# A cross-attention kernel whose media preparation is cut into four chunks and spread over four engines, with part of the value projection behind the first scores

## The reference

```python
qn = layernorm(x, ln_q_g, ln_q_b)
q = qn @ Wq * scale
k, v = jnp.split(media @ Wkv, 2, axis=-1)
sim = jnp.einsum('bhid,bhjd->bhij', q, k)
sim = jnp.where(media_mask[:, None, None, :], sim, neg_inf)
attn = jax.nn.softmax(sim, axis=-1)
out = jnp.einsum('bhij,bhjd->bhid', attn, v)
x = x + jnp.tanh(attn_gate) * attn_out
```

## Time and profile before

| | us |
|---|---|
| median of 3 runs | 939.61 (937.93 to 944.74) |
| the profiled execution, its own time | 945.04 |
| its span | 943.2 |
| TensorE busy | 860.3 (91%) |
| VectorE busy | 610.4 (65%) |
| ScalarE busy | 442.6 (47%) |
| GpSimd busy | 393.1 (42%) |

### The profile page before, as it was taken

How to read it: one execution, slowest core, us unless ns; L and a number is a source line. 1 busy time by engine, 2 the same in 40 slices (tenths; PEclk the granted TensorE clock), 3 DMA queues, 4 the chain that set the end, 5 groups by cost and what they waited for, 6 DMA issues and landing times.

```text
span 943.2 us, 18307 instructions
## 1 busy us (share of the span) xinstructions
PE 860.3 (91%) x7811; PEld 720.0 (76%) x7811; DVE 610.4 (65%) x941; ACT 442.6 (47%) x663; POOL 393.1 (42%) x179
## 2 busy tenths in 40 slices
PE   3589999999999999999999999999998789967996
PEld 2488887788888878888887888888876568846884
DVE  5766798968658888775788868666865132442243
ACT  2255545655445556454554655445544231414141
POOL 0035555556635655555555556635655400000000
PEclk9689999999999999999999999999999899988999
DMA  7100001000000100000000000000024000002000
GB/s 250 33 1 2 1 1 37 1 1 2 1 1 1 36 2 2 2 1 1 2 1 1 2 1 2 1 1 1 2 60 135 1 1 1 1 23 69 0 0 22
DMA packets 19629, 16.61 MB, mean 18 GB/s; under 512 B 849, under 2 KB 18658, under 8 KB 19426
## 3 DMA queue, kind: packets, MB, share of 16 engines
q1 hardware_dynamic: 19554, 15.51, 5.4%
HBM read 14.46 MB, written 1.05 MB: 16 GB/s over the span
## 4 chain that ended last, share of the span: by engine, by line
PE 78%; DVE 11%; ACT 4%; POOL 3%; issue 2%; DMA 2%; SPq 1%; DVEq 0%; POOLq 0%; ACTq 0%
PE psum L910 20%; PE psum L924 16%; PE psum L313 14%; PE psum L881 6%; PE psum L847 4%; PE psum L947 3%; PE psum L980 3%; PE psum L989 3%; PE psum L1035 2%; POOL acc L404 2%; DVE mx L663 2%; PE psum L940 1%; DVE k_lo L656 1%; ACT v L466 1%; DMA wq<-in_L_xattn_Wq_dram 1%
## 5 line engine op out<-in xcount | busy, mean ns | idle before, releaser
L404 POOL TENSOR_TENSOR acc<-acc,ring 128x1024 f32<-128x1024 f32 x128 | 306.5, 2394 | 18.7 <-POOL acc L404 0.4
L663 DVE TENSOR_REDUCE mx<-psum 128x2 f32<-128x800 f32 (+2 forms) x256 | 245.3, 990 | 85.3 <-PE psum L881 77.8
L481 ACT ACTIVATE ring<-psum 128x1024 f32<-128x1024 f32 x192 | 197.0, 1027 | 77.3 <-PE psum L910 71.0
L399 POOL TENSOR_TENSOR acc<-ring 128x1024 f32<-128x1024 f32 x32 | 76.7, 2398 | 322.8 <-ACT ring L481 322.8
L924 PE MATMUL psum<-ring,v 128*64 128x256 f32 (+1 forms) x1664 | 186.7, 381 | 1.8
L924 PEld LDWEIGHTS psum<-ring,v 128*64 128x64 f32 (+1 forms) x1664 | 116.7, 137 | 60.6 <-DVE k_lo L656 3.9
L910 PE MATMUL psum<-nm,maskrow 64*128 64x256 f32 (+1 forms) x832 | 125.9, 298 | 2.2 <-DVE maskrow L645 1.6
L910 PE MATMUL psum<-q_hi,k_hi 64*128 64x256 f32 (+1 forms) x832 | 119.2, 282 | 0.0
L910 PE MATMUL psum<-q_lo,k_hi 64*128 64x256 f32 (+1 forms) x832 | 118.8, 281 | 0.0
L910 PE MATMUL psum<-q_hi,k_lo 64*128 64x256 f32 (+1 forms) x832 | 118.6, 280 | 0.0
L881 PE MATMUL psum<-k_hi,q_hi 64*128 64x400 f32 (+1 forms) x512 | 97.2, 378 | 12.9 <-DVE mx L663 8.3
(11 more groups left out here) (149 smaller groups left out, 1366.6 us busy)
## 6 DMA issues: line engine op xcount, KB each, us to landing
nat<-in_ctx_dram SPq DMA_DIRECT2D x8, 768.0 KB
w<-in_L_xattn_W_dram SPq DMA_DIRECT2D x2, 1024.0 KB, 7.9
xs<-in_x_dram SPq DMA_DIRECT2D x4, 256.0 KB, 5.3
ring<-in_L_xattn_Wkv_dram SPq DMA_DIRECT2D x1, 1024.0 KB, 7.2
wq<-in_L_xattn_Wq_dram SPq DMA_DIRECT2D x1, 1024.0 KB, 9.3
wo<-in_L_xattn_Wo_dram SPq DMA_DIRECT2D x1, 1024.0 KB, 10.3
out_dram<-t_res SPq DMA_DIRECT2D x4, 256.0 KB, 2.2
mask<-in_mask_BxS_bk_dram SPq DMA_DIRECT2D x4, 200.1 KB, 5.9
```

The lines of the kernel that those rows point to most:

```text
L399: nc.gpsimd.tensor_tensor(acc[:, :, :, :], ring[:, 0, :, :, :], ring[:, 1, :, :, :], ALU.add)\
L404: nc.gpsimd.tensor_tensor(acc[:, :, :, :], acc[:, :, :, :], ring[:, g, :, :, :], ALU.add)\
L481: nc.scalar.activation(ring[:, g, :, :, :], score_set[m % 2].rearrange("p (h i q) -> p h i q", h=2, i=2), ACT.Exp).then_inc(S["p_ready"], 1)
L663: nc.vector.tensor_reduce(mx[:, t, :, c], aux_pair[BANK[item] // 2][:, :, 0:min(c1, KEYS) - c0], axis=AX.X, op=ALU.max).then_inc(S["m_max" ...
```

## The change

The media preparation is cut into four chunks of 400 columns (those of K) in place of two halves. The sum over the columns is taken by ScalarE in five parts, each as the accumulator output of a copy of one T part, whose copy (`unread`) nobody reads; VectorE then adds up five numbers. The mixing of the mean is an item of its own (`Y`, four parts), and `P` has four parts. The weights' low parts are made by GpSimd. The mask row is written by ScalarE. K.8.c waits for its own chunk of `mt_lo` and for `wk_lo` alone; V.4 waits for `wv_lo`. The DMA of x and those of the norm rows are issued by ScalarE; SyncE's queue is mask, media, the K half of Wkv, Wq, the V half, Wo. In FIRST, B stands ahead of X, T ahead of W, and G.4 behind P; the maxima M.8 begin between the chunks of K.8; V.4.0 to V.4.2 follow N.8, and G.5 with V.4.3 to V.4.6 are moved behind the first row phase. In the body, Z stands ahead of C and Y.

```diff
-COLUMN_EXTRAS = {2: "B.1", 3: "X.1", 4: "C.1 Z.1", 5: "P.1.0 P.1.1", 7: "I.1"}
+COLUMN_EXTRAS = {2: "B.1", 3: "X.1", 4: "Z.1 C.1 Y.1.0 Y.1.1 Y.1.2 Y.1.3", 5: "P.1.0 P.1.1 P.1.2 P.1.3", 7: "I.1"}
...
-    early = items("X.1 B.1 Z.1 W.1 G.4 T.1.0 T.1.1 T.1.2 T.1.3 T.1.4 C.1 P.1.0 P.1.1")
-    return early + [i for i in ahead if i not in early]
+    early = items("""B.1 X.1 T.1.0 T.1.1 Z.1 T.1.2 T.1.3 T.1.4 W.1 C.1 Y.1.0 Y.1.1 P.1.0 Y.1.2 P.1.1 Y.1.3 P.1.2 P.1.3 G.4
+                     K.8.0 L.8.0 K.8.1 L.8.1 M.8.0 M.8.1 K.8.2 L.8.2 M.8.2 K.8.3 L.8.3 M.8.3 M.8.4 M.8.5 M.8.6 M.8.7 N.8
+                     I.1 V.4.0 V.4.1 K.9.0 L.9.0 V.4.2 K.9.1 L.9.1 R.8 K.9.2 L.9.2 K.9.3 L.9.3""")
+    behind_scores = items("G.5 V.4.3 V.4.4 V.4.5 V.4.6")
+    others = [i for i in ahead if i not in early + behind_scores]
+    cut = others.index(("N", PAIRS + 1))
+    return early + others[:cut] + behind_scores + others[cut:]
...
-    HALVES = [(0, 802), (802, KEYS)]
+    REAL_CHUNKS = [(c0, min(c1, KEYS)) for c0, c1 in CHUNKS]
...
-            sp.dma_start(xs[:, 0, :, :], x_v[0, :, :, :]).then_inc(S["x0_in"], 16)
             sp.dma_start(mask8[:, 0, :], media_mask[0:1, :].broadcast_to([P, KEYS])).then_inc(S["mask0_in"], 16)
             sp.dma_start(nat0[:, 0:KT - 1, :], media_full[0, :, :, :]).then_inc(S["media_in"], 16)
             sp.dma_start(nat0[0:TAIL, KT - 1, :], media_tail[0, :, :]).then_inc(S["media_in"], 16)
-            for i, row in enumerate((ln_q_g, ln_q_b, ln_ff_g, ln_ff_b)):
-                sp.dma_start(normrows[i * DT:(i + 1) * DT, :], row.rearrange("(t p) -> t p", p=P))\
-                    .then_inc(S["norms_in"], 16)
-            sp.dma_start(raw_kv, Wkv).then_inc(S["kv_in"], 16)
+            sp.dma_start(raw_kv[:, 0:INNER], Wkv[:, 0:INNER]).then_inc(S["wk_in"], 16)
             sp.dma_start(wq[:, :, :], Wq.rearrange("(t p) n -> p t n", p=P)).then_inc(S["wq_in"], 16)
+            sp.dma_start(raw_kv[:, INNER:2 * INNER], Wkv[:, INNER:2 * INNER]).then_inc(S["wv_in"], 16)
+            sp.dma_start(wo[:, :, :], Wo.rearrange("(t p) n -> p t n", p=P)).then_inc(S["weights_in"], 16)
+            for i in range(1, BATCH):
...
+            for i, (lo, hi) in enumerate(((wk_lo, wk_hi), (wv_lo, wv_hi))):
+                pool.wait_ge(S["kv_hi"], i + 1)
+                nc.gpsimd.tensor_tensor(lo[:, :], raw_kv[:, i * INNER:(i + 1) * INNER], hi[:, :].bitcast(F32),
+                                        ALU.subtract).then_inc(S["kv_split"], 1)
...
+            act.dma_start(xs[:, 0, :, :], x_v[0, :, :, :]).then_inc(S["x0_in"], 16)
+            for i, row in enumerate((ln_q_g, ln_q_b, ln_ff_g, ln_ff_b)):
+                act.dma_start(normrows[i * DT:(i + 1) * DT, :], row.rearrange("(t p) -> t p", p=P))\
+                    .then_inc(S["norms_in"], 16)
...
-                    if order is FIRST and item == ("T", 1, 0):
-
-                        act.wait_ge(S["kv_in"], 16)
+                    if order is FIRST and item == ("W", 1):
+                        act.wait_ge(S["wk_in"], 16)
                         nc.scalar.copy(wk_hi[:, :], raw_kv[:, 0:INNER]).then_inc(S["kv_hi"], 1)
+                    if order is FIRST and item == ("G", PAIRS // 2):
+                        act.wait_ge(S["wv_in"], 16)
                         nc.scalar.copy(wv_hi[:, :], raw_kv[:, INNER:2 * INNER]).then_inc(S["kv_hi"], 1)
                     if kind in USES_BANK:
                         bank = aux[BANK[item]]
                     if kind == "P":
-                        c0, c1 = HALVES[item[2]]
-                        upto(act, "mt_mixed", b, 2 * n + item[2] + 1)
+                        c0, c1 = REAL_CHUNKS[item[2]]
+                        upto(act, "mt_mixed", b, NCH * n + item[2] + 1)
                         nc.scalar.copy(mt_hi[:, c0:c1], mt[:, c0:c1]).then_inc(S["mt_hi"], 1)
+                    elif kind == "T":
+                        c0, c1 = turned(item[2])
+                        upto(act, "mt_in", b, n * TUNITS + item[2] + 1)
+                        nc.scalar.activation(unread[:, c0:c1], mt[:, c0:c1], ACT.Copy,
+                                             accum_out=part[:, item[2]:item[2] + 1]).then_inc(S["part_in"], 1)
+                    elif kind == "I":
+                        upto(act, "inv_ready", b, n + 1)
+                        upto(act, "s_full", b, n * PER["s_full"])
+                        for r in (slice(32, 64), slice(96, 128)):
+                            last = nc.scalar.activation(maskrow[r, 0:KEYS], inv8[r, :], ACT.Copy, scale=-BIG)
+                        last.then_inc(S["maskrow_ready"], 1)
...
-                    if order is FIRST and item == ("C", 1):
-
-                        for i, (lo, hi) in enumerate(((wk_lo, wk_hi), (wv_lo, wv_hi))):
-                            dve.wait_ge(S["kv_hi"], i + 1)
-                            nc.vector.tensor_tensor(lo[:, :], raw_kv[:, i * INNER:(i + 1) * INNER],
-                                                    hi[:, :].bitcast(F32), ALU.subtract).then_inc(S["kv_split"], 1)
...
-                        upto(dve, "mt_in", b, (n + 1) * TUNITS)
-                        step(nc.vector.reduce_sum(msum[:, 4:5], mt[:, :], axis=AX.X))
+                        upto(dve, "part_in", b, (n + 1) * TUNITS)
+                        step(nc.vector.reduce_sum(msum[:, 4:5], part[:, :], axis=AX.X))
                         step(nc.vector.tensor_scalar(msum[:, 5:6], msum[:, 4:5], msum[:, 3:4], None, ALU.mult))
-                        for c0, c1 in HALVES:
-                            nc.vector.scalar_tensor_tensor(mt[:, c0:c1], inv8[:, c0:c1], msum[:, 5:6], mt[:, c0:c1],
-                                                           ALU.mult, ALU.add).then_inc(S["mt_mixed"], 1)
+                    elif kind == "Y":
+                        c0, c1 = REAL_CHUNKS[item[2]]
+                        nc.vector.scalar_tensor_tensor(mt[:, c0:c1], inv8[:, c0:c1], msum[:, 5:6], mt[:, c0:c1],
+                                                       ALU.mult, ALU.add).then_inc(S["mt_mixed"], 1)
                     elif kind == "P":
-                        c0, c1 = HALVES[item[2]]
-                        upto(dve, "mt_hi", b, 2 * n + item[2] + 1)
+                        c0, c1 = REAL_CHUNKS[item[2]]
+                        upto(dve, "mt_hi", b, NCH * n + item[2] + 1)
                         nc.vector.tensor_tensor(mt_lo[:, c0:c1], mt[:, c0:c1], mt_hi[:, c0:c1].bitcast(F32),
                                                 ALU.subtract).then_inc(S["mt_lo"], 1)
-                    elif kind == "I":
-
-                        if order is FIRST:
-                            dve.wait_ge(S["consts"], 1)
-                        upto(dve, "s_full", b, n * PER["s_full"])
-                        for r in (slice(32, 64), slice(96, 128)):
-                            last = nc.vector.tensor_scalar(maskrow[r, 0:KEYS], inv8[r, :], -BIG, None, ALU.mult)
-                        last.then_inc(S["maskrow_ready"], 1)
...
-                            pe.wait_ge(S["kv_split"], 2)
-                        if n == PAIRS and item[2] % 2 == 0:
-                            upto(pe, "mt_lo", b, 2 * (n // PAIRS) + item[2] // 2 + 1)
+                            pe.wait_ge(S["kv_split"], 1)
+                        if n == PAIRS:
+                            upto(pe, "mt_lo", b, NCH + item[2] + 1)
...
-                            upto(pe, "mt_lo", b, 2 * (n // (PAIRS // 2)) + 2)
+                            upto(pe, "mt_lo", b, NCH + min(u + 1, NCH))
+                            if order is FIRST:
+                                pe.wait_ge(S["kv_split"], 2)
```

16 lines of the change are left out of this document (8 added, 8 removed).

## The result

The changed kernel takes 934.27 us in the median of 11 runs (932.88 to 935.85), the kernel before 944.14 us in the median of 11 runs (937.93 to 947.53). The ratio is 0.9909, with a 95% interval of 0.9884 to 0.9934: 9.9 us faster, just under the 1% line.

The account below looks back on a forecast made before the run. TensorE was taken to bound the bodies, a TensorE-VectorE relay the first 56 us. Start 13.7 + 1.6 - 7.2 + 0.5 = 8.6, plus bodies 1.0, is 9.6 us off the 939.6 median: 930.0 us, forecast 927.5 to 933.5, range 925.5 to 936.5.

Parts of the forecast that it names:

- first rival: Clock and waits eat more: late media or TensorE at half clock from V.4.0 through the row phase; 935 us, chance 0.20.
- The first scores, 13.7 us earlier: Start: the first score product S.8.0 begins at 42.5 us in place of 56.16, bounds 11 and 17 us earlier.
- The collision, 1.5 us in the sum: Start: the second Y on VectorE waits out GpSimd's wk_lo subtraction until 16.6 us, costing 1.5 us.
- "34.5" for the last M.8: Start: the last of the eight maxima ends at 34.5 us against 46.04; S.8.0 starts 8.0 us behind it.
- The row phase, 1.6 gained: First row phase, behind the first scores: 8.8 us at a better clock in place of 10.5, 1.6 us gained.
- Given back, 7.2: Between first row phase and K.10.0: moved G.5 and four V, with their waits, cost 7.2 us (6 to 10).
- The bodies, 1.0 for three: The three bodies: 0.35 us gained in each, 1.0 in all (from 2 lost to 3.5 gained).
- Full phase 3 and its bank waits, 0.75 lost: Bodies: three sums ahead of K.5.0's cast make it 1.3 us late; bank waits pass on 0.75 (0 to 1.3).
- Column phase 4, 1.25 gained: Bodies: two small instructions and four Y replace VectorE's reduction and mixing, so M.6.2 starts 1.25 us earlier.
- Table swaps: Slower rival: ScalarE's accumulator copies among exponentials swap function tables in the bodies, 15.4 us lost; 945.5 us, chance 0.03.
- nothing would be gained at the start: Fourth rival: G.5 and V.4.3 to V.4.6 only move and the chunks gain nothing; 938 to 940 us, chance 0.04.
- The second rival: Better sum in the body: no collision and no passed-on delay of casts, 13.4 us gained; 926 us, chance 0.13.

Follow-up runs that it names:

- weights_on_vector: Changed kernel with the weights' low parts wk_lo and wv_lo made by VectorE in place of GpSimd; 932.92 us, ratio 0.9893 to the kernel before.
- casts_moved: Changed kernel with ScalarE casting wk_hi ahead of its third column sum and wv_hi ahead of the mask row; 931.63 us, ratio 0.9889 to the kernel before.
- start_kept_busy: Changed kernel with products nobody reads filling TensorE's waits between 21 and 36 us; 930.25 us, ratio 0.988 to the kernel before.
- values_ahead: Changed kernel with G.5 and V.4.3 to V.4.6 put back ahead of the first scores; 931.17 us, ratio 0.9868 to the kernel before.
- sums_in_column: Changed kernel with column sums as separate items, in the bodies in column phases 3 and 4, not ahead of K's casts; 932.78 us, ratio 0.9886 to the kernel before.
- padded_1601: Changed kernel with one useless VectorE reduction of 1601 mask bytes ahead of Y.0 in each body; 941.01 us, ratio 0.9978 to the kernel before.
- sums_on_vector: Changed kernel with the column sums back on VectorE as one reduction, at the start and in the bodies; 939.87 us, ratio 0.996 to the kernel before.

## Why the prediction was right, and where it was not

The verdict was right: a gain about at 1%, forecast 9.6 us, measured 9.9, and 934.27 lies in the range. That the two gains are so near each other is luck in part: the start gave 2.2 us less than the sum has, the bodies 3.9 more, and both are told below. The time itself lies outside the forecast's 927.5 to 933.5 and close to the first rival's 935, but that rival had a gain of 4 to 5 us, which did not come. The likeliest time of 930.0 was 4.3 us too low, and that is the base: the forecast took its 9.6 off the 939.61 of three runs, while eleven runs have a median of 944.14. The trace could have warned of it. The 42 runs of the kernel before on the three chips of the experiments fall into two groups by their mean granted clock: 11 runs with 0.972 or more took 938.5 to 940.1 us, 31 with 0.971 or less took 942.2 to 947.8. The profiled execution had 0.969. How many bodies lose the clock behind M.6.2 is likely a part of this, at 1.4 to 2.05 us each in stretch 5 and 0.2 less with stretch 6. It was not followed run by run, and the two falls of the profiled execution are some 3 of the 5.5 us between it and the middle of the upper group. It also means that the change does not gain the same in every run, as the subtraction from the median took for granted: against the upper group the changed kernel is about 5 us faster, against the lower one 8 to 13.

**The first scores, 13.7 us earlier: 11.1.** Up to q_lo the steps held to within 0.7 us. B is one that the sum had too early: it takes B to run from the memsets' end at 4.7, but VectorE waited 0.79 us for the mask, until 5.62, and the first Y ended at 14.8 (14.15 in the sum). The transposes of the media began at 8.60 and VectorE never waited for them; the collision ends at 17.04 (16.6), q_lo at 22.4 (22.1). The collision, 1.5 us in the sum, made the pair of Y 2.1 us longer (3.32 against 1.18 on weights_on_vector); casts_moved got 1.3 of it back. The Trainium skill (GPSIMD Engine Reference, Specifications) names SBUF interfaces that GpSimd shares with VectorE, and contention with VectorE instructions that have two SBUF inputs. The trace agrees: the second Y has two, is recorded as 2.77 us long in place of 0.62, and ends 0.43 us behind GpSimd's instruction. The step that was mis-sized is the next, "34.5" for the last M.8 and "8.0 behind": 35.8 and 9.2. Both are one thing. The sum has no clock in the maxima's part and one between half and full for V.4.0 to R.8 (6.7 us), and it was 0.50 from 24 to 40.5 us; start_kept_busy, at 1.00 there, has 34.5 and 7.0. So the first rival's condition, half clock from V.4.0 on, held up to K.9, and not for the row phase and G.5, which ran at full clock.

**The row phase, 1.6 gained:** 10.49 us became 8.06, from 45.05 to the end of its last product at 53.11, 2.4 gained. **Given back, 7.2:** 7.8, from there to K.10.0 at 60.87: the waits of 0.64 (0.8) and 1.56 (1.6) as forecast, G.5 as forecast, and the V with their bank wait 3.6 in place of 2.9. **negl, 0.5:** K.10.0 to A.8 became 0.66 shorter. The first two miss by 0.8 and 0.6 us and nearly cancel, so the start's 6.4 in place of 8.6 comes from the clock ahead of the first scores. What the prediction did not ask is what the moved items would cost where they had been: values_ahead shows that giving back cost more than the earlier scores brought, by 2.4 us in the profiles.

**The bodies, 1.0 for three: 4.9.** Full phase 3 and its bank waits, 0.75 lost: 0.67 and another 0.29 in stretch 4. The sentence that the delay of phase 4's sums "vanishes in the VectorE wait behind them" was wrong; sums_in_column gets both back. Column phase 4, 1.25 gained: 1.68 in body 1, where the clock stayed. The four P of column phase 5, 0.15 lost: 0.12 in stretch 6 of body 1. The 0.28 in the others is not all theirs: behind a fallen clock stretch 6 is some 0.2 to 0.3 us shorter with either kernel's P (21.64 against 21.91 in padded_1601). And the largest miss: in bodies 2 and 3 the clock fell behind the same wait, 1.42 and 2.05 us more in stretch 5 and 1.2 and 1.9 in the body. I had read the earlier trace rows in body 1 and multiplied by three; the two other bodies were in the same trace. Start 2.2 us less and bodies 3.9 more turn the 9.6 into the 11.3 of the two profiles. The medians have 9.9; the difference is within the spread of the runs of before.

**Rivals.** Table swaps did not come: the changed kernel has five table loads, one at the first instruction and four in the tail, as the kernel before, and the sums run as rows of 0.5 us, with reads of 0.19. That nothing would be gained at the start is refuted by K.8.0. The second rival, a better sum in the body, was right in sign and wrong in its reason: the casts' delay was passed on, and it was the clock that made the body's gain larger.

## What to carry to other kernels

Measure a repeated stretch in every repetition before you multiply it: one wait of TensorE had the same length in three bodies, and the stretch that held it got 1.7, 3.1 and 3.7 us shorter without it, since the clock had fallen behind it in two. An instruction given to GpSimd to relieve VectorE is free only where VectorE has no instruction on two SBUF operands (nor one like z) in the same 2.4 us; move the cast that starts it, and look what it meets next. Where a start is a relay with the matmul engine waiting between short pieces, products that nobody reads may be worth as much as a better order: here 3.7 us at A.8, without moving anything, where the best single change of order gave about 3. And before a gain of 1 us is read off one profile, look how far the same code moves between profiles: here up to 1.5 us at A.8.

## What the runs showed of the hardware

- In work that was otherwise dense, the TensorE clock fell behind a single wait of 1.83 to 2.11 us at M.6.2 in four of nine bodies (before, padded_1601, sums_on_vector), and in none of the 30 bodies of the ten other kernels, where stretch 5 lies between 19.55 and 20.50 us. What decides among the nine is open.
- GpSimd's subtraction of 1024 columns (2.35 us) held not only Y (the pair 3.32 us in place of 1.18), but also z, a scaled copy with one SBUF tensor and two numbers per partition (the pair 2.75 in place of 0.73).
- A ScalarE copy of 384 columns with an accumulator is 0.51 us and its read 0.19, but they overlap the next: three with their reads are 1.63 us in the chain.
- The landing of the first DMA (the mask) moved the whole start by up to 1.5 us between executions (B at 4.99 to 6.50).
- The same code took different times in the tail: from the first A of the last batch to the end it is 348.9 to 352.9 us in the 13 profiles. One place of it is the stretch from A.6 to A.7 of that batch, 16.6 us in four profiles and 17.6 to 17.9 in nine, where the granted clock was 0.50 for a while ahead of A.7 (711.7 to 715.1 us in sums_in_column).
